# 28 matmuls without a reader between the mixing and the first transposes of rows

## The reference, cut to what matters

```python
W = weights[condition]                       # one 128x128 matrix of 16 for each batch
x = x + einsum('bct,bcd->bdt', x, W)         # layer 0: mixes channels
# layer 1: one long convolution for each channel, kernel K of 2048 taps from 64 complex modes
K = 2.0 * einsum('hn,hnl->hl', Ct, exp(P)).real
y = irfft(rfft(x, n) * rfft(K, n), n)[..., :L] + x * D[:, None]
x = x + y * (arange(L)[None, :] < length[:, None])[:, None, :]
```

## Time and profile before

| | |
|---|---|
| median of 3 runs | 1104.42 us |
| profiled execution, its own time | 1108.28 us |
| its span (first to last instruction) | 1106.4 us |
| PE busy | 1008.3 us (91%) |
| DVE, ACT, POOL busy | 624.6, 547.2, 453.2 us |
| granted PE clock, mean | 0.978 of 2.4 GHz |
| HBM traffic | 152.37 MB read, 134.41 MB written |

### The profile page before, as it was taken

The page is one execution under the profiler, slowest core; times in us unless marked ns, Lnnn a source line. Parts: engine busy times, 40 slices in busy tenths (PEclk is TensorE's granted clock), DMA queues, the critical chain, the costliest instruction groups (busy, mean ns, idle before and its releaser), DMA issues.

```text
span 1106.4 us, 24650 instructions
## 1 busy us (share of the span) xinstructions
PE 1008.3 (91%) x9478; PEld 745.8 (67%) x9478; DVE 624.6 (56%) x1518; ACT 547.2 (49%) x1163; POOL 453.2 (41%) x542
## 2 busy tenths in 40 slices
PE   6987789777756999999999999999999999999997
PEld 2332344223214888888888888888888888888886
DVE  6989910000002666666666666666666666666664
ACT  2633344343433555555555555555555555555553
POOL 3211043000203545556556556455455565564520
PEclk9999999899985999999999999999999999999999
DMA  9999999999997698999999999899999999999984
GB/s 336 415 425 422 424 422 418 384 424 424 424 401 216 163 225 227 226 226 228 225 221 226 230 223 227 226 228 215 232 228 221 230 225 231 222 225 229 222 202 115
DMA packets 220227, 305.17 MB, mean 276 GB/s; under 512 B 79874, under 2 KB 178562, under 8 KB 211922
## 3 DMA queue, kind: packets, MB, share of 16 engines
q1 hardware_dynamic: 219426, 302.37, 93.5%
q10 hardware_dynamic: 528, 1.05, 0.3%
q0 software_dynamic: 160, 0.20, 0.1%
HBM read 152.37 MB, written 134.41 MB: 259 GB/s over the span
## 4 chain that ended last, share of the span: by engine, by line
PE 70%; DMA 24%; ACT 4%; issue 1%; SPq 0%; DVE 0%; ACTq 0%
DMA u_scratch<-stage 23%; PE bank L461 23%; PE bank L467 15%; PE bank L426 13%; PE bank L412 10%; PE bank L438 6%; ACT stage L533 3%; PE bank L400 2%; DMA x_f<-in_x 1%; DMA u_row<-u_scratch 0%; DVE st_sb L798 0%; ACT st_sb L554 0%; ACT L505 0%; ACT waves L508 0%; ACT waves L505 0%
## 5 line engine op out<-in xcount | busy, mean ns | idle before, releaser
L461 PE MATMUL bank<-toep,u_t 128*128 128x256 f16 (+1 forms) x3072 | 394.5, 247 | 0.0
L467 PE MATMUL bank<-g_sb,st_sb 128*128 128x256 f16 x1536 | 306.3, 273 | 0.0
L400 PE MATMUL bank<-x_f,w_buf 128*128 128x512 f32 x512 | 242.1, 621 | 63.3 <-ACT stage L533 51.3
L793 DVE SCALAR_TENSOR_TENSOR u_t<-bank,u_t 128x512 f16<-128x512 f32 x256 | 176.4, 689 | 218.5 <-ACT u_t L546 218.5
L461 PEld LDWEIGHTS bank<-toep,u_t 128*128 128x128 f16 x3072 | 280.3, 98 | 24.9
L412 PE MATMUL bank<-ident,u_row 128*128 128x128 f32 x1024 | 280.1, 278 | 16.6 <-DMA u_row<-u_scratch 14.8
L554 ACT ACTIVATE st_sb<-bank 128x128 f16<-128x128 f32 x448 | 123.8, 276 | 296.3 <-PE bank L438 203.7
L798 DVE TENSOR_TENSOR st_sb<-bank,st_sb 128x128 f16<-128x128 f32 x448 | 130.7, 292 | 192.7 <-ACT st_sb L554 190.4
L400 PEld LDWEIGHTS bank<-x_f,w_buf 128*128 128x128 f32 x512 | 96.5, 197 | 204.5 <-issue 112.6
L806 DVE COPY_PREDICATED o_sb<-mask,u_row 128x512 f32<-128x512 uint8 x256 | 213.1, 832 | 16.8 <-issue 16.7
L533 ACT ACTIVATE stage<-bank 128x1024 f32<-128x1024 f32 x128 | 123.9, 1021 | 174.1 <-DMA u_scratch<-stage 157.0
(11 more groups left out here) (118 smaller groups left out, 475.9 us busy)
## 6 DMA issues: line engine op xcount, KB each, us to landing
x_f<-in_x SPq DMA_DIRECT2D x64, 1024.0 KB, 19.6
u_scratch<-stage SPq DMA_DIRECT2D x64, 1024.0 KB, 17.7
u_row<-u_scratch SPq DMA_DIRECT2D x128, 512.0 KB, 5.4
out<-o_sb SPq DMA_DIRECT2D x256, 256.0 KB, 3.8
toep<-k_scratch SPq DMA_DIRECT2D x64, 256.0 KB, 5.4
gt_sb<-g_sb SPq DMA_TRANSPOSE x128, 4.6
nat<-in_L_cond_C SPq DMA_DIRECT2D x2, 64.0 KB, 4.9
k_scratch<-k_body POOLq DMA_DIRECT2D x4, 32.0 KB, 7.1
```

The costliest lines, as they stand in the source:

```text
L400: last = pe.matmul(bank[:, 4 * (n % 2) + k, :], w_buf[n % XS][:, :], x_f[n % XS][:, k * 512:(k + 1) * 512], start=True, stop=True)
L461: pe.matmul(bank[:, y, col + tb * P:col + Q], lhs, t[:, h, b, 0:Q - tb * P], start=first, stop=False, skip_group_check=True)
L467: last = pe.matmul(bank[:, y, col:col + Q], st[:, h, a, gr * ROWS:(gr + 1) * ROWS], g[:, h, b, :], start=False, stop=(m == 2), skip_group_ ...
L793: dve.scalar_tensor_tensor(out=t[:, q // 2, q % 2, 1, :], in0=bank[:, 4 + q, :], scalar=US, in1=t[:, q // 2, q % 2, 0, :], op0=MUL, op1=SU ...
```

## The change

After the 64 batches are mixed, ahead of the transposes of pair 0, PE gets 28 fp32 matmuls of 128x512 with the identity as the stationary operand and a table, `a_re`, as the moving one. They write bank 2, each over the other, and nothing reads what they write; `out_part` of pair 0 overwrites it later. They wait until ACT has copied batch 62 out of banks 0 to 3 (`s_ev` at 126). No other engine's program is changed.

```diff
+WARM = 28
...
+            pe.wait_ge(s_ev, 2 * (NB - 1))
+            for k in range(WARM):
+                pe.matmul(bank[:, 2, :], ident[:, :], ap(a_re, 0, [[1, 512]]), start=True, stop=True)
             pe.wait_ge(s_ev, 2 * NB)
             for k in range(16):
                 transpose_u(0, 0, k)
             pe.wait_ge(s_zero, 1)
```

## The result

The changed kernel took 1113.52 us (median of 6 runs, 1112.01 to 1114.26) against 1105.06 us (6 runs, 1103.63 to 1107.18): a ratio of 1.0076, 95% interval 1.0064 to 1.0088, 8.5 us slower. The forecast was 1110.5, +6.1 us, with a range to 1113.6: the time lies 0.1 us inside the upper bound, and above the 1109.4 to 1111.2 of the likeliest case. The profiled execution took 1112.01 us, its span is 1110.2.

What follows compares the result with a forecast made beforehand. PE was taken to bound the rows stage, so a delay at its start moves the end equally. 11.1 us late, 6.5 given back, 1.5 for the clock's fall: +6.1 us, 1110.5 us, range 1107.6 to 1113.6.

Steps and rivals of the forecast that it cites:

- The filling is longer than the hole: Between mixing and rows: 24.6 us of new matmuls in 13.5 us of idle time, first transpose 11.1 us late.
- M: Start of PE's last mixing matmuls, a mark on the timeline; 318.31 us in the first trace.
- Slot 0 at full clock: From first transpose to slot 1's `inputs_to_state`: 15.3 us at full clock, 6.5 us less than the 21.84 before.
- E: Start of slot 1's 12 `inputs_to_state` matmuls, 358.64 us before; a delay there was to move the end equally.
- The fall in the recurrence: In slot 0's thinly filled recurrence the clock falls again; price 0 to 2.2 us, taken as 1.5.
- What is given back: From first transpose to slot 1's `inputs_to_state`: 6.5 us back (2.1, 2.25 and 2.2), before 1.5 for the clock's fall.
- T: Start of the first transpose of rows, a mark on the timeline; 336.80 us before, forecast at 347.9.
- early fall: Rival: clock falls during the transposes before slot 0's `inputs_to_state`; +9.0 us, 1113.4; chance 0.13.
- The hidden filling: Rival: new matmuls cost half and fit the hole between mixing and rows; 4.8 us earlier, 1099.6; chance 0.05.
- The clock kept throughout: Rival: clock stays up through slot 0, recurrence included; 4.6 us later, 1109.0; chance 0.18.
- half clock: Rival: new matmuls run at half clock, 49 us, slot 1's start some 29 us late, 1133; chance 0.02.

Runs made afterwards that it cites:

- hold28: The change plus one 128x256 matmul without a reader ahead of each of slot 0's six recurrence steps; 1111.29 us.
- w28half: The change with its 28 matmuls at 256 columns in place of 512; 1104.94 us, ratio 1.0005 to the kernel before.
- w0_wait: The change without its new matmuls, only the added wait for batch 62's copy; 1105.45 us, ratio 1.0007 to the kernel before.
- before_again: The kernel before, unedited, timed and profiled once more; 1103.42 us, ratio 0.9994.
- slot0_only: hold28 with no matmuls in the hole, only the six in slot 0's recurrence; 1101.58 us, ratio 0.9972 to the kernel before.
- hold16: hold28 with 16 matmuls in place of 28, and 3 more behind the 16 transposes; 1101.16 us, ratio 0.996 to the kernel before.
- hold16_rows: hold16 with pair 1's rows loaded ahead of `toep`; 1100.65 us, ratio 0.9956 to the kernel before.

## Why the prediction was right, and where it was off

**The filling is longer than the hole: right.** Forecast, 24.6 us from 323.3; measured, 24.1 us from 322.55. PE starts 0.7 us earlier, 0.5 of it because it takes up the filling sooner behind the start of ACT's copies (322.55 - 320.56 = 1.99 us) than the mixing did (2.49), 0.2 because these copies began earlier. The first transpose is at 346.7, 10.1 us behind where the rows would have landed (M + 18.5 = 336.6), for 11.1. The fillings of 20, 28 and 56 confirm the price of one.

**Slot 0 at full clock: right.** Forecast +4.2 us to `inputs_to_state`, measured 350.58 - 346.69 = 3.9, held up by DVE as described; 2.47 to ACT's first copy, measured 2.47; 15.3 to E with the clock kept, measured 15.0 in hold28.

**The fall in the recurrence: right.** It came at 358 us, 11.5 behind the first transpose; its price is 16.1 - 15.0 = 1.1 us in the trace and 1.6 in the medians, for 1.5. With 20 and 56 matmuls it is 1.9 and 2.3 by their traces, so the 1.5 was well placed.

**What is given back: this term was mis-sized.** The sum had 6.5 us, less 1.5 for the fall: 5.0, from the 21.84 us between T and E in the one trace. In the two shorter traces T to E took 17.5 and 18.2 us, so only 1.4 and 2.2 us came back up to the change's 16.1. Term by term: up to `inputs_to_state` the sum had 2.1 us, and 1.1 and 1.3 came back (5.0 and 5.2 us became 3.9), since there pair 1's first transposes had begun 4.1 and 4.7 us behind T and not 5.45. For the 12 matmuls of `inputs_to_state` it had 2.25 us, and nothing came back, since they took 2.43 us already; this is where the sum went wrong most. Behind them it had 2.2 less 1.5 us for the fall, and 0.3 and 0.9 came back. With the two traces the sum is 10.1 for the delay, less 17.9, plus 16.1: +8.3 us, where the medians have +8.5 and +8.2; with traces that lie up to 1.6 us from their medians, the match is not good to better than about 1 us. The start from the median of before was sound; the work given back was read from an execution 3.9 us above that median, and the text noted the difference without asking in which stretch it lay.

**Luck.** The range held by 0.1 us. Its upper bound stood where it did for the early fall of the clock, 1113.4 us, which is also the nearest of the rivals to the measured time; but that fall did not happen in the changed kernel, where the clock is 1.00 from the mixing's end up to 358 us.

**The rivals.** The hidden filling was worth 4.8 us in my working; 14 matmuls gave nothing. One step that failed is that it let PE idle from 339.4 to 342.3 and counted the clock as kept; the other is the same first trace, since 4.8 us under its E is only 1 us under where the two others have it. The ground of the early fall does not hold as it was put: in the run with only the wait nothing but transposes ran on PE from 338.98 us, and the clock rose in the slice from 342. The Trainium skill (TensorE: Matmul & The Clock Gate, "Part 4: PE-mode transpose") says that the full clock does not engage for transpose mode; here the measurement says otherwise for these fp32 transposes (no row tells which mode they ran in). That the clock can fall while they run is shown too, by w28half at 338 us, so this rival was closer than its absence in the changed kernel makes it look. The clock kept throughout needed the six matmuls of hold28, and half clock did not occur. (What I held against that one, 9 tenths and more during the mixing, overlooks a slice at 8 in the earlier trace rows.)

## What to carry to other kernels

A filling for the clock is work like any other: measure the hole in time, from the engine's release to the landing of the data, and count the filling in instructions as the trace has them (here two for each fp32 matmul), since each further microsecond past the landing is lost in full. Look for the place where a slow clock is on the path: here the transposes had slack and filling the hole alone gained nothing, while a recurrence with a half idle PE, followed by dense work, was worth 2.8 us. And where a profiled execution lies well above the median, find the stretch that makes it so, or take a second profile, before pricing a change in it.

## What the runs showed of the hardware that was not expected

- When PE's clock comes back differs between executions whose programs are the same up to there. With the same transposes behind the same 15 us of idle time it rose 3.2 us after the first of them in one trace (w0_wait), 4.2 in another (before_again), 5.7 in a third (slot0_only) and 11.4 in the first. The 29 runs of before in one comparison spread over 6.8 us (1101.44 to 1108.23), the 12 with 20 filling matmuls, in whose trace the clock is held up to the recurrence, over 2.4. No run shows that the clock makes the whole of this difference.
- The clock fell after idle stretches of PE of 1.7 and 2.85 us with transposes between them (the kernel with 14), after one of 1.7 us followed by transposes (w28half), and in the recurrence with PE busy for about half of the time in all ten traces without a filling there. In the four with PE busy for 0.9 of it (hold28, hold16, hold16_rows, slot0_only) it stayed up.
